# Causal mask of the one-head row-maximum units: added by VectorE inside its maximum, in place of a mask matmul on TensorE

## What is computed

```python
c_kv = x @ W_dkv.T
q = (x @ W_dq.T @ W_uq.T).reshape(B, T, nh, hs).transpose(0, 2, 1, 3)
q_lat = jnp.einsum('bhtd,hdl->bhtl', q, k_eff)
attn = jnp.einsum('bhtl,bsl->bhts', q_lat, c_kv) / math.sqrt(hs)
causal_mask = jnp.triu(jnp.ones((T, T), bool), k=1)
attn = jnp.where(causal_mask[None, None], -jnp.inf, attn)
attn = jax.nn.softmax(attn, axis=-1)
```

## Time and profile before

| | us |
|---|---|
| median of 3 runs | 1384.96 (1384.59 to 1385.72) |
| the profiled execution, its own time | 1390.55 |
| its span, first to last instruction | 1388.9 |
| PE busy | 1095.2 (79%) |
| DVE busy | 858.8 (62%) |
| ACT busy | 640.2 (46%) |
| POOL busy | 588.1 (42%) |
| L647, unit scores on PE, 576 | 189.0, mean 393 ns |
| L651, mask matmuls on PE, 384 | 90.4, mean 235 ns |
| L798, one-head maxima on DVE, 512 | 308.4, mean 652 ns |
| q1, the DMA queue of SP and ACT | 163.09 MB |

### The profile page before, as it was taken

How to read it: one execution, slowest core, us unless ns; L and a number is a source line. 1 busy time by engine, 2 the same in 40 slices (tenths; PEclk the granted TensorE clock), 3 DMA queues, 4 the chain that set the end, 5 groups by cost and what they waited for, 6 DMA issues and landing times. The chain is left out here.

```text
span 1388.9 us, 24979 instructions
## 1 busy us (share of the span) xinstructions
PE 1095.2 (79%) x7713; PEld 827.1 (60%) x7713; DVE 858.8 (62%) x2044; ACT 640.2 (46%) x1111; POOL 588.1 (42%) x675
## 2 busy tenths in 40 slices
PE   5957199999999999999981542199999999999900
PEld 3523155555555555555540532199999999999900
DVE  5726188777777777767705863055555555555567
ACT  2620056555555555555672642044444444444444
POOL 4204045555454555545573677212222222322227
PEclk9978599999999999999996555599999999999965
DMA  4954124444444434443234423424244143241173
GB/s 145 378 210 141 51 88 143 146 145 145 145 146 145 145 139 145 142 146 124 93 145 131 159 73 118 159 100 153 64 171 171 45 171 121 90 170 46 45 257 121
DMA packets 93841, 189.92 MB, mean 137 GB/s; under 512 B 27604, under 2 KB 58596, under 8 KB 85508
## 3 DMA queue, kind: packets, MB, share of 16 engines
q1 hardware_dynamic: 82912, 163.09, 33.2%
q0 software_dynamic: 7680, 22.09, 4.6%
q10 hardware_dynamic: 3176, 3.84, 0.9%
HBM read 109.44 MB, written 79.02 MB: 136 GB/s over the span
## 5 line engine op out<-in xcount | busy, mean ns | idle before, releaser
L769 ACT ACTIVATE att_pt<-att_ps_s 128x1024 f32<-128x1024 f32 (+3 forms) x384 | 297.0, 814 | 237.2 <-PE att_ps_s L684 232.8
L798 DVE TENSOR_REDUCE att_pm<-att_ps_m 128x1 f32<-128x512 f32 (+1 forms) x512 | 308.4, 652 | 113.0 <-PE att_ps_m L651 63.9
L1505 ACT ACTIVATE moe_hf<-moe_ps_h,moe_b 128x256 f32<-128x256 f32 x288 | 134.1, 475 | 226.5 <-PE moe_ps_h L1461 222.1
L647 PE MATMUL att_ps_m<-att_k,att_q 128*128 128x512 f32 (+3 forms) x576 | 189.0, 393 | 11.5 <-DVE att_pm L793 10.1
L592 POOL TENSOR_SCALAR_AFFINE_SELECT att_pt<-att_pt 128x512 f32<-128x512 f32 x128 | 81.7, 638 | 252.5 <-ACT att_pt L769 252.5
L684 PE MATMUL att_ps_s<-att_q,att_k 128*128 128x512 f32 (+3 forms) x576 | 168.6, 383 | 17.4 <-DMA att_q<-att_mt 12.1
L1414 POOL DMA_INDIRECT ys<-moe_o,moe_home x72 | 74.2, 1031 | 184.6 <-DVE moe_o L1544 171.7
L684 PEld LDWEIGHTS att_ps_s<-att_q,att_k 128*128 128x128 f32 x576 | 92.3, 194 | 66.3 <-issue 26.9
L1538 DVE TENSOR_TENSOR moe_hTl<-moe_hf,moe_hTh 128x256 fp32r<-128x256 f32 x288 | 124.1, 431 | 9.9
L647 PEld LDWEIGHTS att_ps_m<-att_k,att_q 128*128 128x128 f32 x576 | 106.3, 198 | 38.6 <-issue 12.0
L582 POOL TENSOR_TENSOR att_rec<-att_sums,att_minus 128x16 f32<-128x16 f32 x33 | 95.9, 2907 | 55.8 <-ACT att_sums L755 55.8
(11 more groups left out here) (198 smaller groups left out, 2592.3 us busy)
## 6 DMA issues: line engine op xcount, KB each, us to landing
att_raw<-in_w SPq DMA_DIRECT2D x16, 1024.0 KB, 5.8
ws<-att_raw_hi SPq DMA_DIRECT2D x16, 1024.0 KB, 5.0
ws<-att_raw SPq DMA_DIRECT2D x16, 1024.0 KB, 7.0
moe_rows<-xs SPq DMA_DIRECT2D x38, 258.0 KB
weights_w_0h<-ws SPq DMA_DIRECT2D x8, 1024.0 KB
weights_w_0l<-ws SPq DMA_DIRECT2D x8, 1024.0 KB
att_q<-qs SPq DMA_DIRECT2D x44, 128.0 KB
att_k<-ks SPq DMA_DIRECT2D x44, 128.0 KB
```

Of the source, the lines that this page charges most:

```text
L647: ins = pe.matmul(out[:, end - keys:end], qg[slot][:, h // 2, i * P:(i + 1) * P], kg[slot][:, h, k0:k0 + keys], start=not whole, stop=not ...
L769: act.activation(pt[:, blk % NPT, 2 * p:2 * p + 2, off:CH], ps_s[k % 2][:, :, off:CH], ACT.Exp, scale=HS ** -0.5).then_inc(ex_done, 1)
L798: return dve.tensor_reduce(pm[:, g % 2, place, h:h + 1], src, AX.X, ALU.max)
L1505: act.activation(hf[:, f % NHB], ps_h[f % NHB][:], ACT.Relu, bias=b1[r][:, f:f + 1]).then_inc(hf_done, 1)
```

## The change

The mask constant `future` becomes 512 wide: 384 columns of zeros and then the 128 x 128 triangle. For the 16 one-head units of a group that meet the diagonal (`MASKED`) PE no longer issues L651. DVE no longer takes their maximum with `tensor_reduce` but with one `tensor_tensor_reduce`: it reads the unit from PSUM and the last `keys` columns of `future` (bf16) from SBUF, adds them, writes the sum back over the unit in PSUM, and takes the running maximum from -3e38 up. It becomes two instructions on DVE: the main one and a read of the accumulator into `pm`. Two-head units and the 512 wide mask (L642) stay; they read the last 128 columns of `future`.

```diff
@@ -406,8 +406,11 @@
 UNITS = max_units()
 NU = len(UNITS)
+MASKED = [m for m, (heads, ((i, k0, keys, _), *more)) in enumerate(UNITS)
+          if len(heads) == 1 and k0 + keys == (i + 1) * P]
 HALF = NU // 4 * 2
 NBK = 3
+LOWEST = -3.0e38
@@ -640,15 +643,15 @@
                     if whole:
                         pe.matmul(out[:, 0:squares * P].rearrange("p (s k) -> p s k", k=P), identb[:],
-                                  future[:].unsqueeze(1).to_broadcast([P, squares, P]), start=True, stop=False)
+                                  future[:, CH - P:CH].unsqueeze(1).to_broadcast([P, squares, P]), start=True, stop=False)
                     for n, (i, k0, keys, h) in enumerate(pieces_of):
-                        diag = k0 + keys == (i + 1) * P and not whole
+                        diag = m not in MASKED and k0 + keys == (i + 1) * P and not whole
...
                         if diag:
-                            ins = pe.matmul(out[:, end - P:end], identb[:], future[:], start=False, stop=True)
+                            ins = pe.matmul(out[:, end - P:end], identb[:], future[:, CH - P:CH], start=False, stop=True)
@@ -789,6 +792,9 @@
                     h, src = heads[0], src[:, 0:unit_keys(m)]
+                    if m in MASKED:
+                        return dve.tensor_tensor_reduce(src, src, future[:, CH - keys:CH], 1.0, LOWEST, ALU.add, ALU.max,
+                                                        pm[:, g % 2, place, h:h + 1])
@@ -1577,7 +1583,7 @@
-                "identb": s.sb("identb", [P, P], BF16), "future": s.sb("future", [P, P], BF16)}
+                "identb": s.sb("identb", [P, P], BF16), "future": s.sb("future", [P, CH], BF16)}
@@ -1607,7 +1613,7 @@
-    future = np.triu(np.full((P, P), -1e30, np.float32), 1)
+    future = np.concatenate([np.zeros((P, CH - P), np.float32), np.triu(np.full((P, P), -1e30, np.float32), 1)], axis=1)
```

## The result

| | us | ratio to the kernel before |
|---|---|---|
| kernel before, 8 runs beside it | 1385.01 (1383.03 to 1387.26) | |
| changed kernel, 8 runs | 1388.89 (1387.23 to 1390.89) | 1.0028 [1.0018, 1.0039] |

The change makes the kernel 0.28% slower. I had forecast no change (1383.9 us, within 0.2%); the time lies in the range I gave, but on the side to which I gave 19%. The profiled execution of the changed kernel took 1387.92 us, its span is 1386.3 us. It is shorter than the one profiled execution of before (1388.9 us), whose own time was 5.6 us above its median, so no single pair of spans tells this difference. So I read stages, in three profiles of either kind.

The account below looks back on a forecast made before the run. The prediction took a DMA loop through SP's queue to bound groups 1 to 12, at 35.7 us a group. Terms +0.2, 0, -0.6 and -0.75 gave -1.15 us, so 1384.96 became 1383.9 us, range 1376 to 1392.

Parts of the forecast that it names:

- What bounds the kernel now: Attention, groups 1 to 12: the loop of loads, stores and fetches through SP's queue sets the pace, 35.7 us a group.
- rivals 1 and 2: Groups 1 to 12 each keep 0.6 us, 1376.7 us (13%); or every PE microsecond counts, 1356 us (4%).
- My floor: Attention loop: 35.7 us a group set by transfers, against 30.90 us for a group without a load, set by engines.
- What one mask costs PE: Mask matmuls on PE: 0.12 us each, bounds 0.10 to 0.13, 31 us of PE's time for 256.
- What a masked unit costs DVE: Masked maxima on DVE: +0.10 us a unit, bounds 0 and +0.6.
- Rivals 3 and 4: Masked maximum on DVE: slow, d about 0.6, 1394.6 us (11% for d above 0.45); or locked out by POOL, 1428 us (4%).
- Group 0: Group 0 from 173.74: DVE pays +0.6 us for six masked units, PE saves 0.4 on three masks; sum +0.2 us.
- Groups 1 to 12: The DMA loop sets the pace: PE's 0.6 us a group becomes longer waits, clock falls are covered; 0 us.
- Groups 13 and 14: No load queued from group 13's landing on: -0.6 us in group 13, -0.75 us in group 14.
- the open term: Ahead of group 13: a longer wait might halve PE's clock, 3.5 us of work taking some 1.6 us longer; 1385.5 us.
- The sum: Whole kernel: +0.2 + 0 - 0.6 - 0.75 = -1.15 us, giving 1383.9 us, no change that can be told.
- a loss just beyond 0.2%: Whole kernel: slightly slower than the no-change band, if the clock falls and d, DVE's extra per masked unit, is 0.3; 4%.

Follow-up runs that it names:

- e7: The kernel before, each group's load in the loop bringing one of eight blocks of v (results differ): 1384.29 us, 0.9985; middle stage 412.4 us.
- e18: The changed kernel with each 128 KB copy of q or k from a [2, 16, 1024] source issued as two of [16, 1024]: 1328.64 us, 0.9577.
- e9: The kernel before with each group's load of v in the loop issued by ACT instead of SP: 1387.43 us, 1.0016.
- e2: The changed kernel run again without edits, on the chip of e3 and e4: 1387.95 us, 1.0025.
- e3: The changed kernel with DVE's old plain maximum, so the 256 mask matmuls are gone and nothing replaces them: 1387.87 us, 1.0025.
- e8: The changed kernel, each group's load in the loop bringing one of eight blocks of v: 1387.80 us, 1.0001; middle stage 417.3 us.
- e10: The changed kernel with each group's load of v in the loop issued by ACT instead of SP: 1388.22 us, 1.0023.
- e13: The changed kernel with eight matmuls without a result ahead of PE's wait for the maxima, in groups 2 to 13 only: 1385.46 us, 1.0007.
- e12: The changed kernel with the load of v and, beyond the first group, the maxima's DMAs issued by ACT: 1405.72 us, 1.0160.
- e14: The kernel before with eight matmuls without a result ahead of PE's wait for the maxima, in groups 2 to 13 only: 1386.10 us, 1.0016.
- e5: The changed kernel with eight matmuls without a result ahead of PE's wait for the maxima in every new group: 1391.78 us, 1.0031.
- e6: The kernel before with eight matmuls without a result ahead of PE's wait for the maxima in every new group: 1394.77 us, 1.0048.
- e16: e13 with the masks of groups 0 and 1 left as matmuls on PE: 1383.15 us, 0.9989.
- e17: e16 without the filling matmuls in group 13 (groups 2 to 12 keep them): 1385.20 us, 0.9999.
- e1: The kernel before run again without edits, on the chip of e3 and e4: 1384.78 us, 1.0000.
- e4: The changed kernel with PE's mask matmuls kept as well, so PE and DVE both add the mask: 1384.24 us, 0.9999.
- e15: The changed kernel with DVE adding masks only in groups 14 and 15, all other masks matmuls on PE: 1383.22 us, 0.9990.
- e11: The kernel before with the load of v and, beyond the first group, the maxima's DMAs issued by ACT: 1403.02 us, 1.0122.

## Why the prediction was wrong, step by step

**What bounds the kernel now.** Right that transfers pace groups 1 to 12 and that a PE busy at nine tenths is not the bound: the mean distance of the copies to `mt` stayed at 35.7 to 35.8 us, which also puts rivals 1 and 2 out, and e7 and e18 move it. One of L521 takes 7.47 us to issue, at 524.59; 4.71 was the figure before. Wrong in the place. I read the long issues of L518 as the queue that holds the loop; in e9 they are short and nothing changes. It is 1 MB of q and k in copies that fill an eighth of the DMA engines. The trace of the kernel before had it: from 523 to 531 us, while a load drained, 51 to 58 GB/s moved at a DMA share of 0.13 to 0.15, where the mean of the loop is 142. My floor was wrong too: the group of 30.90 us has fewer units (209 matmuls; the loop has 2732 / 12 = 228 a group). A whole group takes 33.4 us without a long wait, so the loads cost 2.3 us a group and not 4.8.

**What one mask costs PE.** Mis-sized, 0.12 us for 0.06. Group 1 has no long wait and full clock in both kernels, before and after:

```profile
205.46:238.90 33.44, 32.44 (x235) 19.27 (x231) 26.60 (x42) 20.02 (x31) 18.74 (x17) 1.00 0.42 144
```

```profile
205.87:238.84 32.97, 31.49 (x219) 18.71 (x215) 27.17 (x58) 20.07 (x30) 18.70 (x17) 1.00 0.41 144
```

PE is busy 0.95 us less for 16 masks, 0.06 us each. At single places it is 0.04 to 0.085: two units of 384 with their masks took 0.57 us to the next scores (from 507.46 in the earlier trace rows to 508.03), and now take 0.40. Before and after:

```profile
508.03 0.42 PE L684 MATMUL att_ps_s<-att_q,att_k 128*128 128x128 f32 x2
```

```profile
506.98 0.56 PE L650 MATMUL att_ps_m<-att_k,att_q 128*128 128x384 f32 x2
507.38 0.34 PE L687 MATMUL att_ps_s<-att_q,att_k 128*128 128x128 f32 x2
```

My fault was to take a unit of 384 as 0.17 us from its share of the columns, and to give the rest of 0.27 to the mask. The estimate by the Trainium skill (VectorE: DVE Perf Modes, the section on the TRN2 errata), 56 ns, which I had put aside, agrees with what was measured. And half of even that is not seen in the time: the group became 0.47 us shorter (33.44 to 32.97), and PE was idle 0.48 us more, in short waits for ACT and DVE among others.

**What a masked unit costs DVE.** Right and a little high: +0.05 us, forecast +0.10 (the main instruction lasts 0.72 us at 512 where I expected 0.68 to 0.70, and its starts are 0.65 apart, not 0.70). Rivals 3 and 4 are out: no masked unit is slow, and none waits for POOL; L812 still ends with POOL's first L607, as forecast.

**Group 0.** Forecast +0.2, measured +0.6 (33.0 to 33.4, 33.7 and 33.8), with 10.6 to 11.0 us at half clock there instead of 4.1 to 7.2. PE works slowly there behind its long wait. The profiles without mask matmuls in group 0 and without filling there bear on the cause: five with 10.2 to 11.0 us at half clock (after, e2, e3, e8, e10) took 33.4 to 33.8 us, two with 7.9 and 8.0 us (e13, e12) took 32.5 and 32.7. That fits the clock; no run changes the clock of group 0 alone, so it is not shown.

**Groups 1 to 12.** This is the step that failed: "In groups 1 to 12 such a fall is covered." Right was that the waits for the maxima would grow (forecast 30 us, measured 26.7), and that the gain would go there. But a longer wait costs more than itself. PE comes back at half clock for 3.4 or 6.8 us, by the clock's records, and what I called covered is covered only in part. The falls of the kernel before were, on balance: e14 takes them all away and its middle stage stays (426.1 for 426.2 us; its end is 1.5 us shorter, its loop from fetch to fetch as much longer). With the masks gone a fall is more often the long one, and a pair of groups with a long one takes 72.4 us on average where a short one has 71.3. In some of these pairs, groups 10 and 11 of the changed kernel (39.9 + 33.0 = 72.9 us) or groups 4 and 5 of e2 (40.8 + 33.0 = 73.8), the second group takes 33.0 us and has no long wait: the DMAs of its maxima had landed before PE came. PE was late there, and no transfer covered it.

The end of the stage shows the price of a fall in the open. From the last weight fetch to the 14th copy to `mt` it is 20.8 to 21.5 us where the clock did not fall in group 12 (e5, e6, e7, e10, e13, e14, e16, e17, e18), 22.3 to 23.1 where it fell for 3.4 us (before, e1, e2, e4, e8, e9, e15), and 23.6 and 23.8 where it fell for 6.8 us (e3, after). (In e11 and e12 ACT issues the maxima, so they don't compare.) e7, e10 and e18 have no filling, so it is not the filling that makes this short. A fall that nothing covers costs 1.5 to 2.5 us. Measured +3.0 us for the stage where I had 0, and with the filling 4.1 less.

**Groups 13 and 14.** Forecast -1.35, measured -1.1 (means) and -1.3 in e15. The agreement is in part luck: a mask costs half of what I had entered. The clock did not fall there, but in e17 it did, and took the gain of group 13 with it; I had that as the open term.

**The sum.** +0.6 + 3.0 - 1.1 = +2.5 us by stages, +3.2 to 3.9 by the times. I had the mechanism in hand and listed it as a term "open to either side", but priced it for one group only, at 1.6 us, and gave a loss just beyond 0.2% a chance of 4%.

**What stays open.** Of the 3.0 us of the middle stage only 0.3 lie in its end; the other 2.7 are SP's loop from fetch to fetch, 36.0 us in each of the three profiles with the masks gone, and 36.0, 35.6 and 35.7 before. Longer falls are more frequent there, but time at half clock does not order the profiles by itself: the loop takes 35.85 us in e13 and 35.9 in e14 with none, and 35.6 in e1 with 17.1 us. How much of the 2.7 us the clock makes, and how much differs from run to run, these profiles don't tell. Nor was the kernel before run with the split copies; group 1 above says that the change would be worth 0.47 us a group there, some 6 us, but that is worked out and not measured.

## What to carry over

Ask of a wait which engine stands in it and how it comes back: here work taken from TensorE ahead of a wait for a transfer came back as a longer wait, and some of it again as work at half clock. When a loop looks paced by a queue, look at the DMA share while it drains: a share of an eighth is as much as two engines of 16 carry, and splitting the copies was worth more than fifteen times what the change had cost (4.2% and 0.28%). A matmul's price is the change of busy time over a whole group at full clock, not the distance of one pair of starts.

## What the runs showed of the hardware

- Less work on TensorE made the kernel slower: by 0.25% (e3), for some 15 us less of PE's time (256 masks of 0.06 us). Work without a result ahead of the same waits gave 2.5 of 3.5 us back (e13).
- Behind a wait of PE for DMAs the granted clock was at 0.50 for 3.4 or 6.8 us, or stayed at 1.00. Where nothing covered it, a fall of 3.4 us cost about 1.5 us, one of 6.8 us about 2.5 (the end of the middle stage, 18 profiles).
- A read of DVE's accumulator, 141 ns by its record, starts with the next main instruction and adds 0.05 us to the distance of starts at most (0.65 for 0.60 us at 512 elements).
- A DMA that ACT issues instead of SP arrives no sooner when the same DMA engines are held: PE comes out of its wait 9.0 to 10.3 us behind the end of the copy to `mt` in e11, 7.1 to 9.8 in e1.
- Eight copies of 128 KB with a source of [2, 16, 1024] drain at 51 to 59 GB/s and a DMA share of 0.13 to 0.15 (before, e1). As sixteen of [16, 1024], fetch and load together take 14 us at 191 GB/s and a share of 0.80.
